# Softmax denominators of the first attention layer: summing the exponentials on VectorE ahead of one product with ones

## The reference, cut to what matters

```python
q = xt @ Wq.T
qh = q.reshape(B, T, NH, dk).transpose(0, 2, 1, 3)
scores = scale * jnp.einsum('bhqd,bhkd->bhqk', qh, qh)
logits = (scores * cmask + (1.0 - cmask) * NEG) * rmask
attn = jax.nn.softmax(logits, axis=-1)
ctx = jnp.einsum('bhqk,bhkd->bhqd', attn, qh)
out = ctx @ Wo.T
x = x + transpose(out)
```

## Time and profile before

| | before |
|---|---|
| median of 3 runs | 3319.63 us (3316.03 to 3322.01) |
| the profiled execution | 3319.23 us, span 3317.4 us |
| PE busy | 2930.1 us (88%) |
| DVE busy | 1953.0 us (59%) |
| ACT busy | 1254.5 us (38%) |
| layer 0 in the span | about 20 to 818 us |

### The profile page before, as it was taken

The page is one execution under the profiler, slowest core; times in us unless marked ns, Lnnn a source line. Parts: engine busy times, 40 slices in busy tenths (PEclk is TensorE's granted clock), DMA queues, the critical chain, the costliest instruction groups (busy, mean ns, idle before and its releaser), DMA issues. The chain is left out here.

```text
span 3317.4 us, 118574 instructions
## 1 busy us (share of the span) xinstructions
PE 2930.1 (88%) x48920; PEld 1639.8 (49%) x48920; DVE 1953.0 (59%) x4155; ACT 1254.5 (38%) x2019; POOL 644.7 (19%) x717
## 2 busy tenths in 40 slices
PE   6999999996599999999999999389998898888983
PEld 2333333332488888888888888233333232323320
DVE  4555555551776767667676753466666566566650
ACT  1445444443011111111111111136665566656663
POOL 0000000000011212112121211123333343333422
PEclk7999999998799999999999999779999999999996
DMA  1211101111000000000000000144544454554522
GB/s 54 83 47 46 45 26 42 45 36 34 6 0 0 0 0 0 0 0 0 0 0 0 0 0 0 63 123 135 158 141 143 142 155 135 142 151 136 161 58 63
DMA packets 135604, 196.95 MB, mean 59 GB/s; under 512 B 24134, under 2 KB 88870, under 8 KB 129218
## 3 DMA queue, kind: packets, MB, share of 16 engines
q1 hardware_dynamic: 122786, 189.08, 19.4%
q10 hardware_dynamic: 12672, 6.29, 0.6%
HBM read 125.73 MB, written 69.58 MB: 59 GB/s over the span
## 5 line engine op out<-in xcount | busy, mean ns | idle before, releaser
L1289 DVE TENSOR_REDUCE x<-bank 128x1 f32<-128x512 f32 x1024 | 645.0, 684 | 339.4 <-PE bank L1358 338.5
L1213 ACT ACTIVATE x<-exp_ps 128x1024 f32<-128x1024 f32 x512 | 508.6, 1020 | 287.4 <-PE exp_ps L1332 285.2
L807 PE MATMUL exp_ps<-region,gru_hT 128*16 128x128 f32 x16384 | 495.5, 273 | 0.4 <-DVE gru_hT L897 0.4
L1358 PE MATMUL bank<-region 100*128 100x512 bf16 x1024 | 411.1, 404 | 65.3 <-DVE x L1289 40.4
L807 PEld LDWEIGHTS exp_ps<-region,gru_hT 128*16 128x16 f32 x16384 | 431.3, 103 | 19.5 <-DVE gru_hT L897 1.2
L1332 PE MATMUL exp_ps<-region 103*128 103x512 bf16 x1024 | 399.7, 397 | 3.4 <-ACT x L1213 2.3
L869 DVE SCALAR_TENSOR_TENSOR xT<-x,condT,xT (+1 forms) x480 | 358.4, 795 | 0.0
L842 ACT ACTIVATE gru_r<-exp_ps 128x128 f32<-128x128 f32 x256 | 71.2, 278 | 748.6 <-PE exp_ps L807 748.6
L515 DVE TENSOR_REDUCE l_maxes<-exp_ps 128x2 f32<-128x1024 f32 x176 | 215.3, 1225 | 221.3 <-PE exp_ps L576 220.0
L1347 PE MATMUL bank<-x 128*17 128x512 f32 x2048 | 280.2, 620 | 65.1 <-ACT x L1197 64.6
L741 POOL TENSOR_TENSOR xT<-xT,gru_hT 128x64 f32 (+1 forms) x256 | 134.2, 524 | 993.9 <-DVE gru_hT L897 649.2
(11 more groups left out here) (136 smaller groups left out, 3760.9 us busy)
## 6 DMA issues: line engine op xcount, KB each, us to landing
key_query_scratch<-x SPq DMA_DIRECT2D x192, 256.0 KB, 3.4
region<-key_query_scratch SPq DMA_DIRECT2D x64, 768.0 KB
l_rden<-rden_scratch SPq DMA_DIRECT2D x64, 256.0 KB
l_out<-x_scratch SPq DMA_DIRECT2D x64, 192.0 KB
l_xin<-in_x SPq DMA_DIRECT2D x16, 512.0 KB, 4.5
l_rden<-rden_scratch SPq DMA_DIRECT2D x128, 64.0 KB, 2.0
l_xres<-in_x SPq DMA_DIRECT2D x16, 512.0 KB, 3.8
x_scratch<-x SPq DMA_DIRECT2D x16, 512.0 KB, 8.2
```

The source lines that it names most:

```text
L807: last = pe.matmul(out[QW * j:QW * j + rows, cols], hT[:, p, k, 0:rows], wh[:, k, j, gate, :], start=False, stop=True, skip_group_check=True)
L1213: act.activation(probs[:, 2 * (seg % 2) + hp, :, :], exp_ps[slot % 2][:, :, :], ACT.Exp)\
L1289: dve.tensor_reduce(maxes[:, half, qt, head % HH:head % HH + 1], tasks.bank(n)[:, :], AX_X, ALU.max)\
L1358: last = pe.matmul(out, stack[0:KMAX, 1 - par, 1, head, qt * P:qt * P + P], stack[0:KMAX, 1 - par, 0, head, :], start=True, stop=True)
```

## The change

Instead of a product with ones for each of the four tiles of keys of a group, VectorE adds the four exponential tiles up (`add_tile`, three additions of 128 x 1024 fp32 for each pair of heads, in the slots with kt = 1, 2, 3, placed behind the reduction of that slot) into `psum`, a tile in SBUF, and one product with ones is made of the sum. The denominators of group 0 of a step are made in slot 10, those of group 1 in slot 2 of the next step. `probs` has eight buffers. `psum` and `ctx_sb` lie in a part of `region` that the first layer did not use. The turning of the maxima `mta` goes from slot 10 to 9, ACT's copies of the denominators from slots 2 and 10 to 3 and 11, the reciprocal from slot 5 to 7, the two scalings from 9 and 12 to 10 and 13.

```diff
@@ -227,15 +227,19 @@
     scale = 1.0 / math.sqrt(D0)
     SLOTS = 16
 
-    AT = {"mtb": 1, "q1": 3, "v1": 5, "mta": 10, "q0": 11, "v0": 13, "out": 15, "reciprocal": 5, "sums": 10}
-    SCALE = (9, 12)
+    AT = {"mtb": 1, "q1": 3, "v1": 5, "mta": 9, "q0": 11, "v0": 13, "out": 15, "reciprocal": 7, "dens": 2}
+    SCALE = (10, 13)
     SEGS = 8
     NPART = 4
     with ExitStack() as ctx:
         sb = lambda name, shape, dt: ctx.enter_context(nc.sbuf_tensor(name, shape, dt))
         sem = lambda name: ctx.enter_context(nc.semaphore("l0_" + name))
 
-        probs = sb("l0_probs", [P, 4, 2, T], F32)
+        probs = sb("l0_probs", [P, 8, 2, T], F32)
+
+        spare = Arena(g.region[:, 4 * TC * TC * GATES * P:])
+        psum = spare.take([P, GH, T], F32)
+        ctx_sb = spare.take([P, 2, CC, T], F32)
         xin = sb("l0_xin", [P, CC, T], F32)
         xres = sb("l0_xres", [P, CC, T], F32)
         mask_bc = sb("l0_mask_bc", [P, T], F32)
@@ -251,7 +255,6 @@
 
         max_rows = sb("l0_max_rows", [P, 2, T], BF16)
         key_rows = sb("l0_key_rows", [P, 2, T], BF16)
-        ctx_sb = sb("l0_ctx", [P, 2, CC, T], F32)
         den_sb = sb("l0_den", [P, T], F32)
         den_c = sb("l0_den_c", [P, H0 * T // P], F32)
         rden_bc = sb("l0_rden", [P, T], F32)
@@ -271,7 +274,7 @@
         ready = {k: sem(k + "_ready") for k in kinds}
         taken = {k: sem(k + "_taken") for k in kinds}
         kq_done = [sem("kq0_done"), sem("kq1_done")]
-        o_done, pv_done = sem("o_done"), sem("pv_done")
+        o_done, d_done, added = sem("o_done"), sem("d_done"), sem("added")
         split_chain, split_done, masks_set = sem("split_chain"), sem("split_done"), [sem("masks_lo_set"), sem("masks_hi_set")]
         o_taken, d_taken = sem("o_taken"), sem("d_taken")
         recip_done, ctx_ready = sem("recip_done"), sem("ctx_ready")
@@ -409,7 +412,7 @@
             def evac_v(idx, kind, b, par):
                 wait(act, ready[kind], b + 1)
 
-                wait(act, pv_done, SEGS * (b - 2) + 4 * (idx + 1))
+                wait(act, o_done, SEGS * (b - 2) + 4 * (idx + 1))
                 act.activation(v_sb[:, par, :, idx * P:idx * P + P],
                                tasks.bank_of(kind)[:, 0, :].rearrange("p (k o) -> p k o", k=TC), ACT.Copy)\
                    .then_inc(taken[kind], 1)
@@ -432,7 +435,7 @@
 
             def evac_den(s, grp):
 
-                wait(act, pv_done, SEGS * s + 4 * (grp + 1))
+                wait(act, d_done, 2 * s + grp + 1)
                 wait(act, den_stored, 16 * (2 * s + grp))
                 act.activation(den_sb[:, :], d_ps[:, :], ACT.Copy).then_inc(d_taken, 1)
 
@@ -441,15 +444,16 @@
                     seg, hp = slot // 2, slot % 2
                     if active(s, 0):
 
-                        wait(act, pv_done, SEGS * s + seg - 1)
+                        wait(act, o_done, SEGS * s + seg - 3)
+                        wait(act, added, 12 * s + 6 * (seg // 4 - 1) + 2 * max(seg % 4 - 1, 0) + hp + 1)
                         wait(act, ready["st"], 16 * s + slot + 1)
-                        act.activation(probs[:, 2 * (seg % 2) + hp, :, :], tasks.bank_of("st", slot)[:, :, :], ACT.Exp, scale=scale)\
+                        act.activation(probs[:, 2 * (seg % 4) + hp, :, :], tasks.bank_of("st", slot)[:, :, :], ACT.Exp, scale=scale)\
                            .then_inc(taken["st"], 1)
                     if isinstance(s, int) and s in (0, 1):
                         load_gru_weights(SLOTS * s + slot)
                     if slot == 1 and active(s, -1):
                         evac_sums(s - 1, 1 - par, 1)
-                    if slot == 2 and active(s, -1):
+                    if slot == AT["dens"] + 1 and active(s, -1):
                         evac_den(s - 1, 1)
                     if slot == AT["mtb"] and active(s, 0):
                         evac_max(1, "mtb", s)
@@ -459,9 +463,9 @@
                         evac_v(1, "v1", s + 1, 1 - par)
                     if slot == AT["mta"] and active(s, 1):
                         evac_max(0, "mta", s + 1)
-                    if slot == AT["sums"] - 1 and active(s, 0):
+                    if slot == 9 and active(s, 0):
                         evac_sums(s, par, 0)
-                    if slot == AT["sums"] and active(s, 0):
+                    if slot == AT["dens"] + 9 and active(s, 0):
                         evac_den(s, 0)
                     if slot == AT["q0"] and active(s, 2):
                         evac_q(0, "q0", s + 2)
@@ -504,6 +508,20 @@
                 wait(dve, split_chain, 4 * n + 4)
                 dve.tensor_copy(part(2), rest[:, :, :]).then_inc(split_done, 1)
 
+            def add_tile(s, seg, hp):
+
+                grp, kt = seg // 4, seg % 4
+                n = 12 * s + 6 * grp + 2 * (kt - 1) + hp
+                out = psum[:, 2 * hp:2 * hp + 2, :]
+                wait(dve, taken["st"], 16 * s + 2 * seg + hp + 1)
+                if kt == 1:
+
+                    wait(dve, d_done, 2 * s + grp)
+                    dve.tensor_tensor(out, probs[:, hp, :, :], probs[:, 2 + hp, :, :], ALU.add).then_inc(added, 1)
+                else:
+                    wait(dve, added, n - 1)
+                    dve.tensor_tensor(out, out, probs[:, 2 * kt + hp, :, :], ALU.add).then_inc(added, 1)
+
             def step(s, par):
                 for slot in range(SLOTS):
                     if active(s, 1):
@@ -516,6 +534,8 @@
                            .then_inc(taken["max"], 1)
                         if slot % 8 == 7:
                             split(half, "mtb" if half else "mta", s + 1)
+                    if active(s, 0) and slot // 2 % 4:
+                        add_tile(s, slot // 2, slot % 2)
                     for kind, idx, off in (("q1", 1, 1), ("q0", 0, 2)):
                         if slot == AT[kind] and active(s, off):
                             b = s + off
@@ -593,18 +613,16 @@
                 for j in range(GH):
                     h = GH * grp + j
                     last = pe.matmul(o_ps[QW * j:QW * j + QW, :], v_sb[:, par, kt, h * D0:h * D0 + D0],
-                                     probs[:, 2 * (seg % 2) + j // 2, j % 2, :], start=(kt == 0), stop=(kt == TC - 1))
+                                     probs[:, 2 * (seg % 4) + j // 2, j % 2, :], start=(kt == 0), stop=(kt == TC - 1))
                 last.then_inc(o_done, 1)
 
-            def denominators(s, par, seg):
-
-                grp, kt = seg // 4, seg % 4
-                if kt == 0:
-                    wait(pe, d_taken, 2 * s + grp)
+            def denominators(s, grp):
+
+                wait(pe, added, 12 * s + 6 * (grp + 1))
+                wait(pe, d_taken, 2 * s + grp)
                 for j in range(GH):
-                    last = pe.matmul(d_ps[QW * j:QW * j + QW, :], ones[:, :], probs[:, 2 * (seg % 2) + j // 2, j % 2, :],
-                                     start=(kt == 0), stop=(kt == TC - 1))
-                last.then_inc(pv_done, 1)
+                    last = pe.matmul(d_ps[QW * j:QW * j + QW, :], ones[:, :], psum[:, j, :], start=True, stop=True)
+                last.then_inc(d_done, 1)
 
             def task(s, par, n, kind):
                 out = tasks.bank(n)
@@ -651,11 +669,14 @@
                             tasks.free(pe, s, n)
                             task(s, par, n, kind)
                     seg = slot // 2 - 1
-                    part = denominators if slot % 2 else weighted_sums
-                    if seg >= 0 and active(s, 0):
-                        part(s, par, seg)
-                    if seg < 0 and active(s, -1):
-                        part(s - 1, 1 - par, SEGS - 1)
+                    if slot % 2 == 0 and seg >= 0 and active(s, 0):
+                        weighted_sums(s, par, seg)
+                    if slot % 2 == 0 and seg < 0 and active(s, -1):
+                        weighted_sums(s - 1, 1 - par, SEGS - 1)
+                    if slot == AT["dens"] and active(s, -1):
+                        denominators(s - 1, 1)
+                    if slot == AT["dens"] + 8 and active(s, 0):
+                        denominators(s, 0)
 
             pipeline(pe, step, LAST + 1)
```

## The result

| | before | after |
|---|---|---|
| median | 3318.99 us (3316.03 to 3322.01, 4 runs) | 3368.88 us (3366.3 to 3372.4, 4 runs) |
| ratio, 95% interval | | 1.0151 (1.0133 to 1.0169) |
| span and mean granted clock of the profiled execution | 3317.4 us, 0.951 | 3368.6 us, 0.941 |

The forecast was 3331 us, range 3308 to 3346. The direction was right, the size was not: 50 us slower instead of 12.

A forecast was written before the change was run, and what follows sets the result against it. Layer 0 was taken as bound by the exponential's cycle, nearly level with PE; the late xin load makes steps 46.9 us, 0.93 over 45.97, times 13 is 12 us, 3319.2 to 3331; own range 3323 to 3342, with rivals 3308 to 3346.

The forecast's parts named there:

- The bound: Layer 0, slots without an extra task: the exponential's cycle sets 2.31 us a slot, PE's own work is 2.2 to 2.3.
- Rival C: Layer 0: PE is the bound as its busy share says, 96 us less, 3223 us; chance 3%.
- The additions: DVE in layer 0: twelve a step, 1.22 us each, next operation 1.14 behind; slots 14 and 6 lose 0.35 each.
- Rival D: Layer 0: DVE is the bound, additions at 1.36 without overlap, 30 us, 3349 us; chance 10%.
- The denominators behind sums: Slots 2 and 10: priced at 1.00 us each; at 0.87 the sum would be 1.7 us lower.
- The load: Slot 11: xin lands at 46.85 behind the later reciprocal, so the query product waits 2.0 us a step.
- Rival B: Slot 11: the load of xin is in time, step 44.9 and about 0.1, 13 us less, 3307 us; chance 17%.
- first half: Slot 11: PE stands 2.0 us a step for the xin transfer, step 46.9 us, 0.93 more in 13 steps.
- Second half: First steps and tail of layer 0: no such load, PE gains of 1 to 2 us lost again to additions.
- Other layers are not touched: Layers other than layer 0: no change in time.

The follow-up runs named there:

- step 15 filled: Four products of constant data added in each of five odd slots of the last attention step, against the changed kernel: 3375.14 us, ratio to before 1.018.
- reciprocal in 5: The changed kernel with the reciprocal back in slot 5, SP's queue in the old order: 3326.22 us, ratio to before 1.002.

## Why the prediction was right in direction and wrong in size

- **The bound.** That PE's busy time hides the exponential's cycle held: slot 7 to 8 is 2.40 us (forecast 2.31), and without waits for the load and without additions the step is 43.88 (43.9). Rival C (3223 us) had nothing for it.
- **The additions.** 1.22 each, and 0.75 a step on the path (0.7). The places too: above, reduction 13 ends at 437.16 and L596 of slot 14 begins at 437.21, 0.35 us behind the opening of its slot at 436.86. Rival D had nothing for it.
- **The denominators behind sums** begin 0.88 us behind them (402.19 to 403.07), not 1.00. The Trainium skill, TensorEngine Tiling (Array Packing), section Key Properties, on which the 0.87 of the prediction rested, agrees.
- **The load.** The reciprocal comes 22.65 us behind slot 0 (23.0), the product waits 29.7 / 13 = 2.3 us (2.0), 13 times. The three rounds in which the clock held last 46.8 in the mean (46.9). Rival B's step, load in time, is 44.5 to 44.6 (45.0). So the direction was not luck: at 46.8 the 13 steps would have cost 10 us, and the forecast was 12.
- **The step that failed, first half:** "So PE stands 2.0 us a step for a transfer, the new step is 46.9 us". The wait was costed at its length, and the clock at nothing. In the changed kernel the clock falls to 1.2 GHz behind it in 10 of 13 steps, 1.2 to 1.3 us a step in the mean, 14 to 16 us in all. The Trainium skill, TensorE: Matmul & The Clock Gate, section on HAM oscillation, tells of a DMA wait in each round of a loop after which the products run at half the clock. The runs agree, though the waits of its case, 3 to 5 us, are longer than most of these (1.95 to 3.13). I had not weighed it.
- **Second half:** "The first steps and the tail have no such load and come out about even". Step 15 lost 18.6 us. It has no reductions and no score products for maxima, and the change took most of its products with ones; the clock is at half for 44 of its 59.6 us. At least 10 of the 18.6 are the clock (step 15 filled), and it isn't the additions (55.7 without them). At full clock it would take about 40 us by the estimate above (no run shows it alone), so "about even" held for the work and failed for the clock. Step 14 lost most of its 1.6 in the same way: it is 46.2 with 3.4 us of it at half clock, and 44.8 where none is (reciprocal in 5).
- **"Other layers are not touched"** failed by 3.8 us in the GRU, whose code is unchanged. It takes 1218.7 to 1219.7 us in every kernel whose last examples have their denominators by tile, and 1223.5 to 1228.2 in all others, the one without additions included. The extra time is not the clock, which is 1.00 there in all. It sits in single states: in the changed kernel the largest delays, 0.30 to 0.33 us, come behind hidden states 51 and 56 (the first is 0) and again each 32 states later, the length of one pass of VectorE's loop in that layer; without additions they come every fourth state. What makes it so is open.

Together, of the 39 us by which the forecast fell short, steps 2 to 13 are 15.7, step 15 18.6, step 14 1.6 and the GRU 3.8; the rest cancels.

Open as well: why one execution of a kernel keeps the clock in step 15 and the next loses it, and how much of the difference between 10 of 13 steps in the changed kernel and 2 of 13 in the kernel before is the lighter load and how much the longer waits.

## What to carry to other kernels

A wait that is newly put in front of TensorE is to be costed twice: at its length, and at what the products behind it may take at half the clock, with more care where the same change takes work from TensorE. Give that case a chance and a price of its own: here 1.75 us for a round that lost the clock against one that kept it. Look at the granted clock by stretch in the parts with little work before taking their filler away: products that seemed redundant may have held it. And when an operation is moved in a table of slots, follow what stands behind its DMAs in an in-order queue; here two slots' delay of a 0.35 us reciprocal cost more than all that six products of 1 us gave back.

## What the hardware showed that I had not expected

- The clock fell behind waits of 1.95 to 3.13 us in layer 0, with query products of 2.57 to 3.72 us in place of 1.92, and held behind waits of 2.00 and 2.22 us in the same kernel.
- The same kernel ran step 15 in 44.1, 53.3 and 68.2 us in three executions, at granted clocks of 1.00, 0.81 and 0.60 over it.
- Less work took longer: 208 records of products in 59.6 us, where before 256 took 41.0.
